# Two attention and feed-forward layers on one core: another order for the opening loads, norms and weights, an earlier first feed-forward, and four bias additions moved

## The reference, cut to what matters

```python
xn = layernorm(x)
# layer 0: linear attention of 16 heads; out @ o_w.T + o_b
qp, kp = elu(q) + 1, elu(k) + 1
kv = einsum('bhsd,bhse->bhde', kp, v); z = einsum('bhsd,bhd->bhs', qp, kp.sum(axis=2))
attn = einsum('bhsd,bhde->bhse', qp, kv) / (z + 1e-6)
# layer 0: feed-forward with ternary weights: scale = mean(|W|) + 1e-8, W_q = clip(round(W / scale), -1, 1) * scale
ffn = (silu(xn @ wu.T) * (xn @ wg.T)) @ wd.T
x = x + attn @ o_w.T + o_b + ffn
# layer 1: softmax attention of 16 heads with rotary positions, and a feed-forward behind Walsh-Hadamard transforms
xn = layernorm(x)
x = x + softmax(q @ k.T / 4) @ v @ out_w.T + out_b + fwht_ffn(xn)
```

## Time and profile before

| what | us |
|---|---|
| median of 3 runs | 757.34 |
| lowest, highest | 753.59, 758.17 |
| the profiled execution | 757.94 |
| its span in the profile | 756.1 |
| mean granted clock of PE | 0.975 |
| busy: PE, DVE, ACT, POOL | 702.5, 550.8, 419.2, 309.3 |

### The profile page before, as it was taken

How to read it: one execution, slowest core, us unless ns; L and a number is a source line. 1 busy time by engine, 2 the same in 40 slices (tenths; PEclk the granted TensorE clock), 3 DMA queues, 4 the chain that set the end, 5 groups by cost and what they waited for, 6 DMA issues and landing times.

```text
span 756.1 us, 10955 instructions
## 1 busy us (share of the span) xinstructions
PE 702.5 (93%) x4186; PEld 440.5 (58%) x4186; DVE 550.8 (73%) x896; ACT 419.2 (55%) x560; POOL 309.3 (41%) x285
## 2 busy tenths in 40 slices
PE   4778898979988989999999998999999999999998
PEld 3556797968666778777667675333333333333445
DVE  4896766676677846677888887888888188888415
ACT  2242223424534533343232435999999899999883
POOL 1248766344845856244343541121233213422510
PEclk9898999998999999999999998999999999999999
DMA  6127101001104372251301110344434244432221
GB/s 254 56 84 264 56 2 56 1 1 57 55 1 148 119 262 84 84 196 57 103 11 57 56 57 18 130 145 134 145 89 156 92 164 153 137 110 90 89 92 56
DMA packets 25847, 74.13 MB, mean 98 GB/s; under 512 B 4620, under 2 KB 5996, under 8 KB 24964
## 3 DMA queue, kind: packets, MB, share of 16 engines
q1 hardware_dynamic: 21268, 65.37, 25.9%
q0 software_dynamic: 3808, 7.60, 3.4%
q10 hardware_dynamic: 720, 0.48, 0.2%
HBM read 54.54 MB, written 23.06 MB: 103 GB/s over the span
## 4 chain that ended last, share of the span: by engine, by line
PE 60%; POOL 2%; DVE 2%; ACT 1%; issue 1%; DMA 0%; SPq 0%; DVEq 0%; POOLq 0%; ACTq 0%
PE PS L1020 17%; PE PS L758 12%; PE PS L1006 12%; PE PS L764 8%; PE PS L989 6%; PE PS L979 4%; DVE mx L1321 1%; POOL sg L1613 1%; ACT P L1505 1%; POOL rot L1633 1%; POOL rot L1634 1%; DMA scr_k<-spl 0%; PE PS L995 0%; POOL hl L1604 0%; ACT spl L1487 0%
## 5 line engine op out<-in xcount | busy, mean ns | idle before, releaser
L1505 ACT ACTIVATE P<-PS 128x1024 f32<-128x1024 f32 x256 | 249.4, 1025 | 31.6 <-PE PS L1006 31.2
L1328 DVE TENSOR_REDUCE mx<-PS 128x1 f32<-128x512 f32 x300 | 189.2, 683 | 34.5 <-PE PS L989 32.8
L1321 DVE TENSOR_REDUCE mx<-PS 128x2 f32<-128x1024 f32 x106 | 124.8, 1221 | 37.3 <-PE PS L979 37.0
L1020 PE MATMUL PS<-P,VV 128*32 128x512 f32 x1024 | 137.4, 608 | 0.1
L1604 POOL TENSOR_TENSOR hl<-sg,hh 128x512 fp32r<-128x512 f32 x64 | 84.4, 1319 | 120.0 <-ACT hh L1475 67.4
L1006 PEld LDWEIGHTS PS<-QS,KS 64*128 64x128 f32 x512 | 49.0, 185 | 124.0 <-ACT P L1505 110.8
L1006 PE MATMUL PS<-QS,KS 64*128 64x512 f32 x512 | 117.7, 459 | 2.2 <-DVE mx L1321 1.8
L989 PE MATMUL PS<-KM,QM 64*128 64x512 f32 x300 | 82.3, 402 | 0.0
L1461 ACT ACTIVATE sg<-PS,cols 128x512 f32<-128x512 f32 x32 | 22.1, 690 | 81.9 <-PE PS L758 81.9
L1613 POOL TENSOR_TENSOR sg<-sg,us 128x512 f32<-128x512 f32 x32 | 42.1, 1315 | 37.4 <-ACT us L1470 37.4
L758 PE MATMUL PS<-XH,UGH 128*128 128x512 f32 x128 | 54.1, 422 | 1.6 <-ACT sg L1461 0.8
(11 more groups left out here) (208 smaller groups left out, 1406.2 us busy)
## 6 DMA issues: line engine op xcount, KB each, us to landing
QM<-scr_q SPq DMA_DIRECT2D x16, 512.0 KB, 4.3
KM<-scr_k SPq DMA_DIRECT2D x16, 512.0 KB, 5.2
QS<-scr_q SPq DMA_DIRECT2D x16, 512.0 KB, 4.4
KS<-scr_k SPq DMA_DIRECT2D x16, 512.0 KB, 5.2
scr_q<-spl SPq DMA_DIRECT2D x24, 256.0 KB, 3.4
scr_k<-spl SPq DMA_DIRECT2D x24, 256.0 KB, 3.5
scr_o<-OE POOLq DMA_DIRECT2D x14, 256.0 KB, 2.7
stg<-in_tern SPq DMA_DIRECT2D x3, 1024.0 KB, 4.8
```

Source lines behind the costliest of these rows:

```text
L1020: i = e.matmul(PS[32 * c:32 * c + 32, 7, :], v_head(8 * b + kt, 2 * j + c // 2), P[s % 4][:, chunk(c // 2 + 2 * (c % 2))], start=(kt == 0) ...
L1321: e.tensor_reduce(mx[p % 2][:, :, qt, half], PS[:, b:b + 2, :], AX.X, ALU.max).then_inc(q["mx"], 2)
L1328: e.tensor_reduce(mx[p % 2][:, h, qt, half:half + 1], bank[b], AX.X, ALU.max).then_inc(q["mx"], 1)
L1505: e.activation(P[s % 4][:, half * 1024:(half + 1) * 1024], PS[:, b:b + 2, :].rearrange("p b n -> p (b n)"), ACT.Exp).then_inc(q["ex"], 1)
```

## The change

It does this:

- SP issues all opening loads at once: token blocks 0 and 1, wa0, the output bias, blocks 2 and 3, the three ternary matrices, each with a staging buffer of its own (numbers 2 and 3 lie over the later hh, hl and AH, AL; the normed blocks 2 and 3 move to other addresses). The load of the down weights and the padding writes follow when W0L is done.
- W0L is made on POOL, in two pieces: the key and value columns, then the query and output columns in two instructions.
- The norms of blocks 2 and 3 and the ternary weights are put in a new order: TU and TG before the weave, TD and both norms beside its first eight pieces (`beside`).
- The weave begins after five side pieces (four `kv_in`, one `q0`), and deals one side piece for each main piece instead of 0.8.
- `kv_sum` runs two tiles behind `kv_in` instead of one, and `kv_end` yields five times instead of once.
- The value bias is no longer added to each tile: ACT copies ve, and `kv_sums` adds bias times the sum of the keys, with two more DVE instructions and two waits between.
- The gate waits for TU alone, the first up for TG; the first tanh no longer waits for the norm of block 3.
- The biases of layer 1 are added by POOL in block 0 of its own feed-forward, at main pieces 4, 12, 20 and 28. The norm of its block 2 begins at piece 2 of the last block of layer 0 instead of 8.

```diff
-FIRST = 12
-RATE0 = 0.8
+RATE0 = 1.0
...
-        put("tern_scale", n, ps.next())
+        put("tern_scale", n, pf.next())
...
         put("kv_in", tt, ps.next())
-        if tt % 8 > 0:
-            put("kv_sum", tt - 1)
+        if tt % 8 > 1:
+            put("kv_sum", tt - 2)
         yield
         if tt % 8 > 2:
             put("kv_out", tt - 3)
 
     def kv_end(b):
+        put("kv_sum", 8 * b + 6)
+        yield
         put("kv_sum", 8 * b + 7)
+        yield
         for tt in range(8 * b + 5, 8 * b + 8):
             put("kv_out", tt)
+        yield
         put("kv_sums", b)
+        yield
         yield
...
     def ln1(c, ring):
...
-        put("bias", 1, c)
...
-            if 14 <= n < 18:
-                next(tn)
-                if n == 17:
-                    put("scales")
-                    put("spread_vb")
-                    put("load_wa1")
+            if n == 15:
+                put("scales")
+                put("spread_vb")
+                put("load_ob1")
+                put("load_wa1")
...
+    def beside(sides):
+
+        front = [(tn[2], 2), (ln0[2], 1), (tn[2], 1), (tn[2], 1), (ln0[2], 1), (tn[2], 1), (ln0[3], 1), (ln0[3], 1)]
+        for n, _ in enumerate(sides):
+            if n < len(front):
+                step(*front[n])
+            if n in (4, 16):
+                put("bias", 0, 2 + n // 16)
+            yield
+
+
+    NORMS = {(0, 2, 2): 0, (0, 2, 10): 1, (0, 3, 2): 2, (1, 0, 5): 3}
 
     def main(layer):
         norm = iter(())
                     next(norm, None)
                 if (layer, c, k) == (0, 3, 0):
                     put("load_cs")
+                if layer and c == 0 and k in (4, 12, 20, 28):
+                    put("bias", 1, k // 8)
...
     put("start")
-    put("load_wa0")
     ln0 = [layernorm(c, pf) for c in range(NCH)]
-    for i in (0, 1, 0):
-        next(ln0[i])
+    tn = [ternary(n) for n in range(3)]
+    sd0 = side0()
+
+    def step(work, count=1):
+        for _ in range(count):
+            next(work, None)
+
+    step(ln0[0])
+    step(ln0[1])
+    step(ln0[0])
     put("w0h")
-    for i in (0, 1):
-        next(ln0[i])
-    put("w0l")
-    for i in (1, 2):
-        next(ln0[i])
+    step(ln0[1])
+    put("w0l", 0)
+    step(ln0[0])
+    step(ln0[1])
+    put("w0l", 1)
+    step(tn[0], 2)
+    put("load_down")
     put("signs")
-    sd0 = side0()
-    next(sd0)
-    next(ln0[2])
-    next(tn)
-    next(sd0)
-    next(ln0[2])
-    next(ln0[3])
-    for n in range(FIRST):
-        if n < 10:
-            next(tn)
-        next(sd0)
-        if n < 2:
-            next(ln0[3])
-        if n > 7:
-            put("bias", 0, n - 8)
+    put("bias", 0, 0)
+    step(sd0)
+    step(tn[0])
+    step(ln0[2])
+    step(tn[0])
+    step(tn[1], 2)
+    step(tn[0])
     put("half")
-    put("load_down")
-    put("load_ob1")
-    weave(main(0), sd0, RATE0)
+    step(sd0)
+    step(tn[1])
+    step(sd0)
+    step(tn[1])
+    step(sd0)
+    step(tn[1])
+    step(sd0)
+    step(ln0[3])
+    put("bias", 0, 1)
+    weave(main(0), beside(sd0), RATE0)
...
-        stg = [sb(f"stg{i}", 174 + 8 * i, [128, 2048]) for i in range(2)]
-        XC = [sb(f"XC{i}", (190, 194, 156, 160)[i], [128, 4, 256]) for i in range(4)]
+        stg = [sb(f"stg{i}", (174, 182, 156, 147)[i], [128, 2048]) for i in range(4)]
+        XC = [sb(f"XC{i}", (190, 194, 16, 20)[i], [128, 4, 256]) for i in range(4)]
...
-        STAGE = {"wa0": (0, 16), "tern0": (1, 16), "tern1": (0, 32), "tern2": (1, 32), "down": (0, 48), "wa1": (1, 64),
-                 "up": (0, 64)}
+        STAGE = {"wa0": (0, 16), "tern0": (1, 16), "tern1": (2, 16), "tern2": (3, 16), "down": (0, 32), "wa1": (1, 48),
+                 "up": (0, 48)}
...
             def start():
-                for c in range(NCH):
+                def tokens(c):
                     e.dma_start(X[:, 4 * c:4 * c + 4, :], x_d[:, 4 * c:4 * c + 4, :]).then_inc(d[f"x{c}"], 16)
 
-            def load_wa0():
+                tokens(0)
+                tokens(1)
                 e.dma_start(stg[0][:, :], wa0).then_inc(d["st0"], 16)
                 e.dma_start(OB[:, :], ob_d[0]).then_inc(d["ob"], 16)
+                tokens(2)
+                tokens(3)
+                for n in range(3):
+                    i, _ = STAGE[f"tern{n}"]
+                    e.dma_start(stg[i][:, :], tern[n]).then_inc(d[f"st{i}"], 16)
 
             def load_ob1():
                 e.wait_ge(q["bx"], 4)
                 e.dma_start(OB[:, :], ob_d[1]).then_inc(d["ob"], 16)
 
-            def tern_abs(n):
-                if n == 1:
-                    e.wait_ge(q["w0l"], 1)
-                if n == 2:
-                    e.wait_ge(q["tt"], 2)
-                i, _ = STAGE[f"tern{n}"]
-                e.dma_start(stg[i][:, :], tern[n]).then_inc(d[f"st{i}"], 16)
-
             def load_down():
-                e.wait_ge(q["tt"], 4)
+                e.wait_ge(q["w0l"], 3)
...
             def load_wa1():
-                e.wait_ge(q["tt"], 6)
+                e.wait_ge(q["tt"], 2)
...
             def gate(layer, c, m, b):
...
-                        e.wait_ge(q["tt"], 4)
+                        e.wait_ge(q["tt"], 2)
...
             def up(layer, c, m, b):
...
+                    if m == 0 and c == 0:
+                        e.wait_ge(q["tt"], 4)
...
@block.vector
-                e.tensor_tensor(ve[j][:, :, 0:128], bank[b][:, 256:512].rearrange("p (g n) -> p g n", g=2),
-                                BKV[:, 256:512].rearrange("p (g n) -> p g n", g=2), ALU.add).then_inc(q["kvv"], 1)
 
             def kv_sums(b):
                 e.wait_ge(q["kvo"], 8 * (b + 1))
                 if b:
                     e.wait_ge(q["an"], 8)
                 for g in range(2):
-                    e.tensor_tensor(kvb[g][:, 0:128], bank[2][:, g * 129:g * 129 + 128], MASK[:, :], ALU.mult)
-                    i = e.tensor_scalar(kvb[g][:, 128:136], MASK[:, 0:128:16], bank[2][:, g * 129 + 128:g * 129 + 129], None, ALU.mult)
+                    total = bank[2][:, g * 129 + 128:g * 129 + 129]
+                    e.tensor_scalar(kvb[g][:, 128:136], MASK[:, 0:128:16], total, None, ALU.mult)
+                    e.scalar_tensor_tensor(kvb[g][:, 0:128], BKV[:, 256 + g * 128:384 + g * 128], total, bank[2][:, g * 129:g * 129 + 128],
+                                           ALU.mult, ALU.add).then_inc(q["kvb"], 1)
+                for g in range(2):
+                    e.wait_ge(q["kvb"], 2 * b + g + 1)
+                    i = e.tensor_tensor(kvb[g][:, 0:128], kvb[g][:, 0:128], MASK[:, :], ALU.mult)
                 i.then_inc(q["kvs"], 1)
...
@block.scalar
             def kv_in(tt, b):
                 j = tt % 4
+                e.wait_ge(q["kvz"], tt + 1)
+                if tt >= 4:
+                    e.wait_ge(q["kvo"], tt - 3)
+                e.activation(ve[j][:, :, 0:128], bank[b][:, 256:512].rearrange("p (g n) -> p g n", g=2), ACT.Copy).then_inc(q["kvv"], 1)
+
+            def kv_sum(tt):
+                j = tt % 4
                 e.wait_ge(q["kvm"], tt + 1)
                 e.activation(ek[j][:, :], ek[j][:, :], ACT.Exp).then_inc(q["kve"], 1)
...
             def att_t(c, m, b):
...
+                if h == 0:
+                    e.wait_ge(q["tt"], 6)
...
             def gate(layer, c, m, b):
...
-                    e.wait_ge(q["lnl"], 8)
...
@block.gpsimd
+            def w0l(i):
+
+                raw = stg[0][:, :].rearrange("p (k n) -> p k n", k=2)
+                e.wait_ge(q["w0h"], 1)
+                for cs in ((slice(256, 768),), (slice(0, 256), slice(768, 1024)))[i]:
+                    e.tensor_tensor(W0L[:, :, cs], raw[:, :, cs], r32(W0H[:, :, cs]), ALU.subtract).then_inc(q["w0l"], 1)
```

24 lines of the change are left out of this document (11 added, 13 removed).

## The result

The changed kernel takes 762.4 us (median of 7 runs, 759.6 to 764.0) against 757.6 (median of 7) for the kernel before on the same chip: ratio 1.0066 (95% interval 1.0042 to 1.0089), 5 us slower, where 748.5 was forecast. The profiled execution took 761.4 (span 759.6).

A forecast was written before the change was run, and what follows sets the result against it. Gain only before 242: DVE bounds the start, PE is full later. Terms 4.8 + 4.3 + 2.2 - 2.0 + 1.5 - 2.0 = 8.8 take the profiled 757.94 to 749.1, median 748.5; 8-in-10 range 740 to 757.

The forecast's parts named there:

- Part 1: Head: earlier wa0 and W0L on POOL in halves bring the first key/value matmul to 14.5 instead of 19.9.
- POOL has nothing else there: Head: besides W0L's first half, POOL has only the second half and the first bias, then the first ek.
- Part 2: Front to kv_sums(0) done: DVE-limited, state 6.3 us late with 11.1 us of PE work moved forward, +4.8 (0 to +11).
- 1.0 for waits that stay: Front: allowance of 1.0 us for waits, added to DVE's work and contention, putting kv_sums(0) done at 66.6.
- rival C: Front: POOL holds DVE, 25 operations cost 22 us instead of 5.5; 765.5, or 768 with half-clock matmuls; chance 0.07.
- Parts 3: From 72 to 83: PE waits and slow matmuls go because the third ternary matrix TD is done earlier, +4.3 (0 to 5.3).
- part 4: kv_end: five yields put main pieces into the 2.23 us wait at 130.89, +2.2 (1 to 2.2).
- Part 5: Denser side, 1.0 instead of 0.8: the norm of block 1 now pays a wait for its turn, -2.0 (0 to -4.2).
- the projection: Last query/key half moves from layer 1 into layer 0; no PE work saved, so no term.
- Part 6: Second layer's biases: four POOL additions leave layer 0 (+1.5) and arrive in layer 1's first block (-2.0, to -7.1).
- relief of 1.5 in layer 0: Layer 0: four bias additions of 2.38 us leave POOL, worth +1.5 (0 to 4).
- My warning sign: From 242 on: the prediction is wrong if POOL releases more than 5 us of PE's waits.

The follow-up runs named there:

- b_load: Kernel before with only the loads reordered: first weights and biases ahead of the third and fourth token blocks; W0L stays on DVE: 754.6 us, ratio 0.9959.
- a_exp: Changed kernel with ACT's exponential of a tile's ek one piece earlier, ahead of the copy of the newest ve: 759.3 us, ratio 1.0041 to the kernel before.
- a_kv_end: Changed kernel with kv_end in one step again, no main pieces between the last kv_sum and what waits for it: 767.2 us, ratio 1.013 to the kernel before.
- a_tail: Changed kernel with 0.8 instead of 1.0 side pieces per main piece in layer 0's last block: 765.5 us, ratio 1.0108 to the kernel before.
- a_norm_bias: Changed kernel with block 2's norm back at piece 8 and layer 1's biases back behind their norms: 756.8 us, ratio 0.9995 to the kernel before.
- a_dense: Changed kernel with 1.15 instead of 1.0 side pieces per main piece in layer 0's last block: 754.3 us, ratio 0.9967 to the kernel before.
- a_w0l: Changed kernel with W0L computed on DVE instead of POOL, same three cuts and places: 763.5 us, ratio 1.0095 to the kernel before.

## Why the prediction was wrong, point by point

- **Part 1, head (first matmul 14.5): right in eight executions of fifteen.** In the changed kernel's it came at 15.98, in eight others with the same head at 14.0 to 14.2. The loads brought 3.0 of it (b_load, 16.96 for 19.91); the halves of W0L cost POOL 2.34, 1.31 and 1.27 as I took them, but "POOL has nothing else there" looked at POOL alone: where DVE loses the start, the first half blocks a norm slice for its whole length, 1.9 us. TU and TG came at about 26 and 33 instead of 24 and 31.
- **Part 2, front (+4.8): failed, +0.2.** The sum of DVE's work was near (48.3 forecast, 46.6 measured), but by two errors that offset: contention was oversized (kv_sum 0.72, not 1.07; norm slices 0.55, not 0.65: 2.0 for my 5.5), and the rest was 1.8 short, 1.3 of it the XL of the second block, which does fall into the window (16.78). The step that failed is "and 1.0 for waits that stay": DVE idles 58.0 - 46.6 = 11.4 us, 7.1 of it behind an exponential that the change itself had moved behind another operation of ACT. I counted what the edit took from DVE (ve, -3.3) and not what it put ahead of the exponential. That state is reached at 73.3, past the 72 which I had tied to rival C, but not by C's mechanism: DVE is idle, not held. a_exp bears out part of this only: with half of that idle time gone the state comes some 2 us earlier, so what the other half and the remaining 4.3 us of idle time are worth is open.
- **Parts 3 (+4.3) and 4 (+2.2): right**, +5.1 and +2.1 in the windows; a_kv_end shows that in the changed kernel part 4 is worth 4.8, since without it PE waits 6.0 us in front for the first sequence.
- **Part 5 (-2.0, bounds 0 to -4.2): failed, -8.3; this is most of the miss.** Block 2 cost 1.7 for my 2.0, and the wait that I named is there: the norm of block 1 now pays 1.64 for its turn and 0.38 for the bank, 2.0. That the block's sum agrees is luck all the same: the norm of block 0 pays 1.4 less than before (1.47 + 1.30 for 2.84 + 1.36), the clock takes 1.5 less and small waits at products and weights of 1.8 are gone, while PE waits 4.4 us at pieces of the attention (behind `at` and `QP`), which my sum did not have. The step that failed is block 3, which alone lost 6.6 and for which my sum has nothing. The early norm of block 2, six pieces forward, had no term at all; moving it back by three pieces gives 6.4. And the projection was priced at nothing because "no PE work is saved": I counted PE's work only, while with it rotations and splits came among the products of block 3, ahead of what PE needed next (the wait of 4.4). Its price is one of place and not of amount: still more of it in block 3 (1.15) gives 7.5, less of it (a_tail) costs 3.2 more.
- **Part 6 (-0.5, bounds to -5.6): right kind, size off.** The biases cost 2.5 to 2.8 in three comparisons; there was no relief of 1.5 in layer 0: before, PE had no wait behind POOL there from 61 to 242 that the profile lists. Beside the late norm (a_norm_bias) nothing was measured.
- **Sum.** The miss is 4.6 in part 2, 6.3 in part 5, 1.7 in part 6, less 0.7 in parts 3 and 4: 11.9 of the 12.3 between 749.1 and the 761.4 of the profiled execution. Won were 7.4 for my 11.3, lost 10.5 for my 2.5. My warning sign, POOL as releaser of over 5 us from 242 on, came almost true (4.4 directly, 3.2 through ACT).
- **Open:** how much of a_dense's 7.5 is the clock (6.0 in its one profile) and how much order, as no run keeps one and changes the other; what W0L on POOL is worth alone, since a_w0l moves the first bias too; and whether one kernel has the early or the late head in all its executions.

## What to carry to other kernels

When a side stream is woven denser into a main one, what counts is not the work it brings but which of its instructions now stands directly ahead of one that TensorE needs: list for each engine the queue ahead of the next product, and try two or three densities and places, since here three pieces of one norm moved the end by 6.4 us, a density of 1.15 instead of 1.0 by 7.5, and 1.3 instead of 1.15 lost 12.0. When an operation is moved between engines, write down the new queue order of the engine that receives it, and look for a loop in which engine A waits for B's second operation, whose first waits for A. Try the cheapest part alone first: the load order by itself brought 3.1 us. And before a trace is read as the effect of an edit, compare the stretch ahead of the edit: where that differs, as the head does here by 1.9 us, the number holds more than the edit.
